# A tuned two-layer scan and FFN kernel: expert masks and sign sums on GpSimd, the sign transposes by DMA, the last slot in two halves

## The chip, the cores and the metric

The kernel runs on one core of a Trainium2 chip. The metric is the device time of one execution in microseconds; the kernel before takes 103.62 us, the median of three runs (103.58 to 103.7). The profile shows the four compute engines of the core (TensorE or PE, VectorE or DVE, ScalarE or ACT, GpSimd or POOL) and SyncE (SP), which here only issues DMAs. Each engine takes its instructions in the order in which the program lists them, and waits on semaphores.

## The reference, cut to what matters

`x` and `F` are (4, 256, 256) in float32, four slots `b` of 256 time steps and 256 channels. There are two layers:

```
x = x + moe(wkv(x, F, F, w0, u0, cond))           # layer 0
x = x + ffn(wkv(x, F, F, w1, u1, cond))           # layer 1

wkv(r, k, v): a_t = a_{t-1}*decay + exp(k_t)*v_t,  b_t = b_{t-1}*decay + exp(k_t)   forward and in reverse
              num = af + ab - ekv + euk*v,  den = bf + bb - ek + euk
              out = sigmoid(r) * num / max(den, 1e-8) * (0.8 + 0.2*tf)
moe(h):       gate = argmax softmax(h Wg^T) over 8 experts; y = 4 * prob * B_e (A_e h), rank 64
ffn(h):       gelu(h W1q^T + b1) W2q^T + b2,   Wq = sign(w) where |w| >= 0.7*mean|w|, else 0
```

`W1` is 1024 x 256 and `W2` is 256 x 1024.

## The kernel before, in words

The channels lie on the partitions, in two chunks `c` of 128, and time lies on the free axis. All work is cut by layer `l` (0, 1) and slot `b` (0 to 3); each engine has its own list of calls, written out by hand, and every order below is that of such a list. There is no planner; semaphores with counts join the lists.

- **Front.** SyncE loads F, x, gate and expert weights, `w1` and `w2` (`w_nat`, 1 MB each). TensorE transposes F, x, A, B against an identity `ident`; between them stand `warm_up` and `keep_warm`, transposes of the identity with no result.
- **wkv of one layer and slot.** On VectorE: `forward(l, b, q)` and `backward(l, b, q)`, two scans each (one per chunk), for the numerator (NUM) and the denominator (DEN); `own_keys`; `add_den`; then ScalarE makes a reciprocal as exp(-ln) (`log_den`, `reciprocal`), and VectorE refines it in one step (`den_times_rec`, then `ratio`, or `refine_rec` and `product` where the numerator comes late). GpSimd does `own_values`, `add_num`, `times_sigmoid` (layer 0) or `times_tanh` (layer 1), `num_times_rec` (needed only for `ratio`) and `seed`, a tiny product that starts the reverse scan.
- **moe of one slot.** TensorE `gate_logits`; VectorE `gate`, `gate_index`; ScalarE `gate_exp`; VectorE `expert_mask`, a reciprocal and two compares of 128x128, one per half of the time steps (lines 882 to 893), with the expert numbers and both scalars in PSUM; TensorE `transpose_mask`; ScalarE `copy_mask`; TensorE `expert_in` into banks 0 and 1; VectorE `select_expert`; TensorE `place_residual` (the slot's x, by matmul with the identity) and `expert_out` on top of it; ScalarE `keep_x1`. `tanh` on ScalarE gives the gate of layer 1 (as tanh, in the table set of gelu; each change of table set is a load).
- **Weights.** ScalarE sums |w| (`abs_sum`), TensorE and VectorE turn that into a threshold, ScalarE writes two sign matrices in bf16, `above` and `below`, 128x2048 per weight matrix. TensorE adds and transposes them in one go, `transpose_weights(k)`, eight groups of eight bf16 matmuls (lines 1182 to 1198) through one PSUM bank, and ScalarE takes each group out as its sign (`evacuate_wT`).
- **ffn of one slot.** The input is split in a high and a low part (`xin_high`, `xin_low`). TensorE `hidden(b, j)`, j = 0 to 3, eight matmuls of 128x128x256; ScalarE `gelus`; `h_high`, `h_low`; TensorE `place_output(b)` (x1 + b2, by matmul with the identity) and `ffn_out(b, j, n)`, four matmuls each; `result` copies the bank out and SyncE stores it.

TensorE's list goes from `warm_up` at line 1266 to the last `ffn_out` at 1372, with `hidden(0, 0)` at 1318. The two lines on which the placements rest are:

```
pe.matmul(bank[Y_BANK][...], x_nat[...], ident[:, :], start=(c == 0 and n == 0), stop=False)      # 1130
pe.matmul(o_region(b, n)[...], x1T(b)[...], ident[:, :], start=(...), stop=False)                 # 1250
```

Of the kernel before, what the change touches and what calls it, by code (L numbers as in the profile page):

```python
# [14 lines left out]
P = 128  # L15
# [9 lines left out]
def adaln_ffn_kernel(nc, x, fside, cond, w_l0, u_l0, A, Bw, Wg, w_l1, u_l1, w1, b1, w2, b2, out):  # L25
# [23 lines left out]
    with ExitStack() as ctx:  # L49
# [9 lines left out]
        identb = sb("identb", [P, P], BF16)  # L59
# [32 lines left out]
        above2 = sb("above2", [P, NC, DFF], BF16)  # L92
        wsum = sb("wsum", [P, 2])
# [7 lines left out]
        gsum = sb("gsum", [P, NI])  # L101
        mask = sb("mask", [P, 2 * NT, P])
# [32 lines left out]
        consts_ready, identb_ready = sem("consts_ready"), sem("identb_ready")  # L135
# [21 lines left out]
        below_ready, above_ready = sem("below_ready"), sem("above_ready")  # L157
        qT_psum, wT_ready = sem("qT_psum"), sem("wT_ready")
# [23 lines left out]

        NEG_AT, IDX_AT, GREC_AT, EXPERT_AT = 4 * ND, 4 * ND + 2, 4 * ND + 2 + NI, P
# [5 lines left out]
        expert_ps = bank[DVE_BANK][:, EXPERT_AT:EXPERT_AT + P]  # L189
# [85 lines left out]

        def seed(eng, l, b, q):
# [25 lines left out]

        def copy_on(eng, dst, src):
# [10 lines left out]
        def h_high(eng, b, j):  # L314
# [24 lines left out]
        def _(sp):  # L339
# [29 lines left out]
            sp.dma_start(w2_nat[:, :, :], w2.rearrange("(n p) f -> p n f", p=P)).then_inc(w_loaded[1], 16)  # L369
            for b in range(NB - 1):  # L370
# [10 lines left out]
        def _(pool):  # L381
# [24 lines left out]

            def factors():
# [36 lines left out]
            seed(pool, 0, 2, NUM)
            add_num(pool, 0, 2)
            times_sigmoid(pool, 2)
            num_times_rec(0, 2)
            seed(pool, 0, 3, NUM)
            own_values(pool, 1, 0)
            add_one(0)  # L450
            seed(pool, 1, 0, NUM)
            add_num(pool, 0, 3)
            times_sigmoid(pool, 3)
            seed(pool, 1, 0, DEN)
            num_times_rec(0, 3)
            add_num(pool, 1, 0)
            times_tanh(pool, 0)
            add_b2(0)
            num_times_rec(1, 0)
            seed(pool, 1, 1, DEN)  # L460
            add_b2(1)
            own_values(pool, 1, 1)
# [935 lines left out]
```

## Time and profile before

| what | value |
|---|---|
| median of three runs | 103.62 us |
| the profiled execution | 102.58 us |
| its span, first to last instruction | 100.8 us |
| PE busy | 93.5 us, 93% |
| DVE busy | 86.7 us, 86% |
| ACT busy | 80.2 us, 80% |
| POOL busy | 66.1 us, 66% |
| DMA | 6.43 MB, nearly all in the first 20 us |

Busy time counts an instruction from its start to its end, and the ends of pipelined matmuls overlap the next ones; how long a group holds its engine is best read from the start of the group to the start of the next. The table's shares are means over two stages that have different limits. A chain of waits is followed back from the last instruction, at each step to what released it.

### The profile page before, as it was taken

The page shows a single profiled execution, that of the slowest core. Times are in us where ns is not written, and L with a number is a line of the kernel's source. Part 1 is how long each engine was busy: PE and PEld are TensorE (multiplying, and loading weights), DVE is VectorE, ACT ScalarE, POOL GpSimd, SP SyncE. Part 2 cuts the span into 40 slices and gives each one's busy share as a digit, 9 for nine tenths or more (in the row PEclk, how much of TensorE's full clock was granted, in tenths as well). Part 3 has the DMA queues.
Part 4 walks back from the last instruction along what each step waited for, and adds up shares of the span by engine and source line. Part 5 has one row for each costly group of instructions (what it writes and reads, how often), then busy time and mean ns, then how long its engine had stood idle before and what let it go on. Part 6 is the DMA issues. An engine that isn't in the chain of part 4 may idle for free. (4 is left out here: it accounts for less than half of the span.)

```text
span 100.8 us, 2134 instructions
## 1 busy us (share of the span) xinstructions
PE 93.5 (93%) x665; PEld 85.0 (84%) x665; DVE 86.7 (86%) x203; ACT 80.2 (80%) x144; POOL 66.1 (66%) x90
## 2 busy tenths in 40 slices
PE   3999779989988999999999999999999999999980
PEld 2688659978878889888888888989999999999970
DVE  3389999999999999999999999999997997883330
ACT  4369999999986679999667499998986899986520
POOL 4058679979984796069868987999980867005310
DMA  1899999700000000000000000000000020200005
GB/s 33 243 292 336 298 228 385 281 3 0 3 0 0 3 0 7 0 0 0 0 3 7 0 0 0 0 0 0 0 7 0 0 104 33 72 7 3 0 0 208
DMA packets 6886, 6.43 MB, mean 64 GB/s; under 512 B 2370, under 2 KB 6492, under 8 KB 6876
## 3 DMA queue, kind: packets, MB, share of 16 engines
q1 hardware_dynamic: 6868, 6.31, 20.2%
q8 instruction: 5, 0.08, 0.3%
q14 instruction: 5, 0.04, 0.1%
q10 hardware_dynamic: 8, 0.00, 0.0%
HBM read 5.26 MB, written 1.05 MB: 63 GB/s over the span
## 5 line engine op out<-in xcount | busy, mean ns | idle before, releaser
L298 POOL TENSOR_TENSOR h_lo<-h,h_hi 128x512 fp32r<-128x512 f32 x9 | 12.3, 1367 | 12.5 <-DVE h_hi L306 7.1
L794 DVE TENSOR_TENSOR_SCAN run<-bank,kv 128x256 f32<-128x256 f32 x32 | 20.1, 674 | 0.2
L1156 PE MATMUL bank<-num,AT 128*128 128x256 f32 x64 | 15.5, 384 | 0.7 <-DVE hm L900 0.5
L1258 PE MATMUL bank<-w2T,h_hi 128*128 128x256 f32 x64 | 15.9, 286 | 0.0
L611 ACT ACTIVATE h<-bank,bT 128x256 f32<-128x256 f32 x32 | 13.1, 478 | 3.2 <-PE bank L1224 2.9
L1224 PE MATMUL bank<-xin_hi,w1T 128*128 128x256 f32 x64 | 15.5, 283 | 0.0
L1258 PE MATMUL bank<-w2T,h_lo 128*128 128x256 f32 x64 | 15.6, 281 | 0.0
L1224 PE MATMUL bank<-xin_lo,w1T 128*128 128x256 f32 x64 | 15.2, 277 | 0.0
L1172 PE MATMUL bank<-hm,BT 128*128 128x256 f32 x64 | 14.6, 381 | 0.0
L1156 PEld LDWEIGHTS bank<-num,AT 128*128 128x128 f32 x64 | 11.6, 190 | 2.2 <-issue 0.9
L1172 PEld LDWEIGHTS bank<-hm,BT 128*128 128x128 f32 x64 | 11.9, 190 | 1.5
L1224 PEld LDWEIGHTS bank<-xin_hi,w1T 128*128 128x128 f32 x64 | 12.0, 188 | 0.6 <-POOL xin_lo L292 0.4
L248 POOL TENSOR_TENSOR num<-num,own 128x512 f32<-128x512 f32 x7 | 8.9, 1278 | 5.2 <-DVE num L828 5.1
L1258 PEld LDWEIGHTS bank<-w2T,h_lo 128*128 128x128 f32 x64 | 12.0, 188 | 0.0
L1258 PEld LDWEIGHTS bank<-w2T,h_hi 128*128 128x128 f32 x64 | 12.0, 188 | 0.0
L1224 PEld LDWEIGHTS bank<-xin_lo,w1T 128*128 128x128 f32 x64 | 12.0, 188 | 0.0
L242 POOL TENSOR_TENSOR own<-own,vs 128x512 f32<-128x512 f32 x8 | 10.2, 1275 | 1.4 <-DVE own L778 1.3
L828 DVE TENSOR_TENSOR_SCAN bank<-bank,run 128x256 f32<-128x256 f32 x16 | 10.2, 681 | 0.0
L828 DVE TENSOR_TENSOR_SCAN num<-bank,run 128x256 f32<-128x256 f32 x16 | 10.1, 671 | 0.0
L405 POOL TENSOR_TENSOR num<-num,run 128x512 f32<-128x512 f32 x5 | 6.4, 1279 | 1.2 <-DVE run L794 0.9
L529 ACT ACTIVATE run<-bank 128x512 f32<-128x512 f32 x8 | 4.8, 605 | 2.9 <-DVE bank L835 2.9
L305 ACT ACTIVATE h_hi<-h 128x512 fp32r<-128x512 f32 x11 | 6.8, 635 | 0.3 <-ACT h L611 0.2
(141 smaller groups left out, 226.1 us busy)
## 6 DMA issues: line engine op xcount, KB each, us to landing
w_nat<-in_L_ffn_w_dram SPq DMA_DIRECT2D x2, 1024.0 KB, 8.5
F_nat<-in_fside_BxSxS_dram SPq DMA_DIRECT2D x4, 256.0 KB, 3.1
x_nat<-in_x_dram SPq DMA_DIRECT2D x4, 256.0 KB, 4.9
out_dram<-outb SPq DMA_DIRECT2D x3, 256.0 KB, 2.1
A_nat<-in_L_ffn_A_dram SPq DMA_DIRECT2D x1, 512.0 KB, 5.6
B_nat<-in_L_ffn_Bw_dram SPq DMA_DIRECT2D x2, 256.0 KB, 6.3
out_dram<-outb SPq DMA_DIRECT2D x2, 128.0 KB, 1.9
wv_rows<-in_L_cond_w_dram SPq DMA_DIRECT2D x2, 1.0 KB
```

The lines of the kernel that those rows point to most:

```text
L242: eng.tensor_tensor(own[:, r, :, NUM, :], own[:, r, :, DEN, :], vs[:, b], ALU.mult).then_inc(ownv_ready[r], 1)
L248: eng.tensor_tensor(num_at(l, b), num_at(l, b), own[:, r, :, NUM, :], ALU.add).then_inc(num_ready[r], 1)
L298: eng.tensor_tensor(h_lo[:, b % 2, 2 * j:2 * j + 2], h32[:, b % 2, 2 * j:2 * j + 2], h_hi[:, b % 2, 2 * j:2 * j + 2].bitcast(F32), ALU.sub ...
L305: return eng.activation(dst, src, ACT.Copy)
L405: pool.tensor_tensor(num_at(l, b), num_at(l, b), run[:, r, :, DEN, :], ALU.mult).then_inc(q_ready[r], 1)
L611: act.activation(h32[:, b % 2, f], bank[g_bank[NJ * b + j]][:, (f % 2) * T:(f % 2 + 1) * T], ACT.Gelu, bias=bT[:, f:f + 1], scale=0.5).the ...
L794: dve.tensor_tensor_scan(run[:, r, c, q], decay_ps[:, l, c, b:b + 1].broadcast_to([P, T]), kv[:, b, c, q], 0.0, ALU.mult, ALU.add).then_in ...
L828: dve.tensor_tensor_scan(into[:, c, ::-1], decay_ps[:, l, c, b:b + 1].broadcast_to([P, T]), run[:, r, c, q, ::-1], 0.0, ALU.mult, ALU.add) ...
L1156: mm = pe.matmul(bank[H_BANK + k][:, (m % 2) * T:(m % 2 + 1) * T], AT[:, c, m * P:(m + 1) * P], num_at(0, b)[:, c], start=(c == 0), stop=( ...
L1172: mm = pe.matmul(bank[Y_BANK][:, o * T:(o + 1) * T], BT[:, m, o * P:(o + 1) * P], hm[:, b % 2, m], start=False, stop=(o == NC - 1 and m == ...
L1224: mm = pe.matmul(bank[g_bank[g]][:, (f % 2) * T:(f % 2 + 1) * T], w1T[:, c, f * P:(f + 1) * P], part[:, b % 2, c], start=(c == 0 and part ...
L1258: mm = pe.matmul(o_region(b, n), part[:, b % 2, f, n * P:(n + 1) * P], w2T[:, f], start=False, stop=(f == NF - 1 and part is h_lo and (n = ...
```

## The change

1. The expert mask moves from VectorE to GpSimd. The expert numbers and scalars now lie in SBUF. The reciprocal stays on VectorE as `gate_reciprocal`.
2. GpSimd adds `above` and `below`, eight pieces of 128x512 in bf16 (`add_signs(w, q)`). SyncE transposes each sum, 128x2048, by one DMA from SBUF to SBUF, and ScalarE evacuates it in two steps of 1024 columns. The 64 matmuls of `transpose_weights` are gone; 28 transposes of the identity (`fill`) and other counts of `warm_up` and `keep_warm` are in.
3. `place_residual` and `place_output` become transposes (`is_transpose=True`).
4. For the last slot of layer 1 everything from the reverse scan of the denominator to `xin_low` is done by chunk, `last_hidden(j, c)` by input chunk, and the last hidden group's gelu, high and low part and output by 128 features. The second chunk's denominator lies in another bank.
5. The lists of all four engines are in a new order. Some calls change the engine: `times_tanh(2)`, `xin_high` of slot 1, `add_num(1, 2)`, several `h_high` and `h_low`, `result(0)`. Ten table loads stand where twelve stood.

```diff
+        def add_signs(w, q):
+            nc.gpsimd.wait_ge(above_ready, w + 1)
+            nc.gpsimd.wait_ge(below_ready, w + 1)
+            part = slice(q * 2 * C, (q + 1) * 2 * C)
+            signs = (above1 if w == 0 else above2)[:, :, :].rearrange(flat)[:, part]
+            nc.gpsimd.tensor_tensor(signs, signs, below[:, part], ALU.add).then_inc(signs_added, 1)
...
+            for w, signs in enumerate((above1, above2)):            # SyncE, ahead of the stores
+                sp.wait_ge(signs_added, 4 * (w + 1))
+                sp.dma_start(signsT[:, w], signs[:, :, :].rearrange(flat), transpose=True).then_inc(signs_moved[w], 16)
...
+            def expert_mask(b):                                     # GpSimd
+                pool.wait_ge(consts_ready, 4 + NE)
+                pool.wait_ge(index_steps, (NT + 1) * (b + 1))
+                pool.wait_ge(grec_ready, b + 1)
+                if b >= 2:
+                    pool.wait_ge(mask_psum, b - 1)
+                for i in range(NT * b, NT * (b + 1)):
+                    pool.tensor_scalar(mask[:, i % (2 * NT)], expert_of[:, :], chosen[:, i:i + 1], prob[:, i:i + 1],
+                                       ALU.is_equal, ALU.mult).then_inc(mask_ready, 1)
...
             def sign_below(k):
                 act.wait_ge(thr_ready, 2)
                 if k:
-                    act.wait_ge(qT_psum, 4)
+                    act.wait_ge(signs_added, 4)
...
             def evacuate_wT(k):
-                act.wait_ge(qT_psum, k + 1)
+                act.wait_ge(signs_moved[k // 2], 16)
...
+                act.activation(dst, src, ACT.Sign).then_inc(wT_ready, 1)      # 128x1024, src = signsT
...
GpSimd's list, from num_times_rec(0, 1) on:
+            expert_mask(0)
+            add_signs(0, 0)
+            add_num(pool, 0, 2)
+            add_signs(0, 1)
             seed(pool, 0, 3, DEN)
+            add_signs(0, 2)
+            add_signs(0, 3)
+            expert_mask(1)
             times_sigmoid(pool, 2)
+            add_signs(1, 0)
             seed(pool, 0, 3, NUM)
+            add_signs(1, 1)
+            seed(pool, 1, 0, NUM)
+            add_signs(1, 2)
+            add_num(pool, 0, 3)
+            add_signs(1, 3)
+            seed(pool, 1, 0, DEN)
+            times_sigmoid(pool, 3)
+            expert_mask(2)
+            num_times_rec(0, 3)
...
ScalarE's list, from reciprocal(0, 1) on (the order after the change):
             gate_exp(0), evacuate_B(0), evacuate_B(1), sign_above(0), sign_below(0), log_den(0, 2), copy_mask(0),
             reciprocal(0, 2), sign_above(1), gate_exp(1), sign_below(1), copy_mask(1), keep_x1(0), log_den(0, 3),
             reciprocal(0, 3), gate_exp(2), evacuate_wT(0), [table] tanh(0), keep_x1(1), tanh(1), evacuate_wT(1),
             copy_mask(2), [table] log_den(1, 0), reciprocal(1, 0), gate_exp(3), evacuate_wT(2), keep_x1(2),
             xin_high(0), evacuate_wT(3), copy_mask(3), log_den(1, 1), reciprocal(1, 1), [table] gelus(0, 0) ...
...
TensorE's list:
-            keep_warm(19)
-            transpose_B(1)
-            keep_warm(27)
+            keep_warm(40)
             gate_logits(0)
+            expert_in(0, 0)
             weight_totals()
+            transpose_B(1)
+            fill(9)
+            place_residual(0)
             expert_in(0, 1)
+            fill(14)
             transpose_mask(0)
+            fill(5)
             gate_logits(1)
...
-            transpose_weights(0)            # and 1 to 7, further down
...
+            expert_out(2)
             expert_in(3, 0)
+            transpose_mask(3)
             expert_in(3, 1)
             hidden(0, 0)
...
+            place_output(3)
+            last_hidden(0, 0)
+            last_hidden(1, 0)
+            last_hidden(0, 1)
+            last_hidden(2, 0)
+            last_hidden(1, 1)
             ffn_out(2, 2, 0)
             ffn_out(2, 2, 1)
+            last_hidden(2, 1)
...
+            last_ffn_out(6, 0)
+            last_ffn_out(6, 1)
+            last_ffn_out(7, 0)
+            last_ffn_out(7, 1)
```

VectorE's list, in the stretch that the prediction adds up (from line 911 on; the order after the change): `seed(0, 0, NUM)`, `own_keys(0, 0)`, `backward(0, 0, DEN)` and `NUM`, `own_keys(0, 2)` and `(0, 1)`, `add_den(0, 0)`, `forward(0, 1, NUM)`, `backward(0, 1, DEN)`, `own_keys(0, 3)`, `den_times_rec(0, 0)`, `add_den(0, 1)`, a seed, `ratio(0, 0)`, `backward(0, 1, NUM)`, `forward(0, 2, NUM)`, `gate(0)`, `forward(0, 2, DEN)`, `thresholds`, and so on to `select_expert(2, 1)`, `(2, 0)`, `add_den(1, 0)`, `forward(1, 1, DEN)`, `gate(3)`, `den_times_rec(1, 0)`, `gate_index(3)`, `gate_reciprocal(3)`, `refine_rec(1, 0)`, a seed, `product(1, 0)`. Ahead of that point it has, unlike before, `own_keys(1, 1)`, `forward(1, 1, NUM)`, and `refine_rec` with `product` for slot 2 of layer 0.

## Rows read from the trace of the kernel before

**Rows 1.** The page: busy time, share of the span and instructions of each engine

```profile
PE 93.5 (93%) x665; PEld 85.0 (84%) x665; DVE 86.7 (86%) x203; ACT 80.2 (80%) x144; POOL 66.1 (66%) x90
```

**Rows 2.** Chain that ended last: start, us, what (the last two: the timeline)

```profile
61.02 0.44 PE bank L1163 x2
97.84 0.42 DVE outb L306
86.37 0.69 DVE L292 TENSOR_TENSOR xin_lo<-sig,xin_hi 128x512 fp32r<-128x512 f32 x1
87.24 0.37 PE L1224 MATMUL bank<-xin_hi,w1T 128*128 128x256 f32 x1
```

**Rows 3.** Stretches: length, busy us of each engine (instructions), clock, DMA

```profile
10.31:54.66 44.35, 41.87 (x293) 37.33 (x293) 43.72 (x117) 38.83 (x66) 33.85 (x37) 1.00 0.22 67
58.70:97.90 39.20, 38.88 (x315) 37.79 (x314) 31.94 (x60) 32.54 (x62) 23.65 (x22) 1.00 0.04 14
15.00:20.00 5.00, 5.00 (x46) 4.91 (x46) 5.00 (x9) 5.00 (x10) 4.92 (x5) 1.00 0.93 344
```

**Rows 4.** Timeline of VectorE: start, us, engine, line, operation, tiles, count

```profile
10.31 1.27 DVE L828 TENSOR_TENSOR_SCAN bank<-bank,run 128x256 f32<-128x256 f32 x2
11.48 0.86 DVE L778 SCALAR_TENSOR_TENSOR own<-ek_raw,bank 128x256 f32<-128x256 f32 x2
...
25.79 0.16 DVE L886 RECIPROCAL bank<-gsum 128x2 f32<-128x2 f32 x1
...
26.73 0.68 DVE L857 SCALAR_TENSOR_TENSOR num<-bank,num 128x512 f32<-128x512 f32 x1
...
51.38 1.26 DVE L794 TENSOR_TENSOR_SCAN run<-bank,kv 128x256 f32<-128x256 f32 x2
...
74.48 0.23 DVE L286 TENSOR_TENSOR run<-run,bank 128x2 f32<-128x2 f32 x2
```

**Rows 5.** Timeline of TensorE: the same columns

```profile
8.96 2.60 PE L1090 MATMUL bank<-ident,x_nat 128*128 128x128 f32 x12
...
15.35 2.24 PE L1041 MATMUL bank<-ident 128*128 128x128 f32 x19
...
24.88 1.05 PE L1130 MATMUL bank<-ident,x_nat 128*128 128x128 f32 x8
25.77 1.89 PE L1156 MATMUL bank<-num,AT 128*128 128x256 f32 x8
...
52.89 3.67 PE L1172 MATMUL bank<-hm,BT 128*128 128x256 f32 x16
56.40 0.22 PE L1196 MATMUL bank<-identb,above 128*128 128x128 bf16 x1
...
56.85 1.95 PE L1156 MATMUL bank<-num,AT 128*128 128x256 f32 x8
```

**Rows 6.** Groups of ScalarE by line and shape: count, busy us, mean ns

```profile
L580 ACT ACTIVATE above<-w_nat,thr 128x2048 bf16<-128x2048 f32 x2 | 4.0, 1990 | 0.0
L595 ACT ACTIVATE w2T<-bank 128x512 fp32r<-128x512 f32 x4 | 2.4, 590 | 0.5 <-PE bank L1197 0.5
L621 ACT ACT_TABLE_LOAD x1 | 1.3, 1283 | 0.0
```

**Rows 7.** Groups of GpSimd by line and shape: the same columns

```profile
L242 POOL TENSOR_TENSOR own<-own,vs 128x512 f32<-128x512 f32 x8 | 10.2, 1275 | 1.4 <-DVE own L778 1.3
L227 POOL TENSOR_SCALAR kv<-ek_raw 128x512 f32<-128x512 f32 x2 | 1.2, 612 | 0.7 <-ACT ek_raw L509 0.6
L231 POOL TENSOR_SCALAR kv<-ek_raw 128x256 f32<-128x256 f32 x2 | 0.8, 400 | 3.2 <-ACT ek_raw L513 3.2
```

**Rows 8.** DMA issues: tiles, count, KB each, median us from issue to landing

```profile
out_dram<-outb SPq DMA_DIRECT2D x3, 256.0 KB, 2.1
A_nat<-in_L_ffn_A_dram SPq DMA_DIRECT2D x1, 512.0 KB, 5.6
B_nat<-in_L_ffn_Bw_dram SPq DMA_DIRECT2D x2, 256.0 KB, 6.3
```

More of the change, by code:

```diff
@@ L450, in _ @@
+            seed(pool, 1, 1, NUM)
             add_one(0)
[L451 to L456, printed above, removed]
-            times_tanh(pool, 0)
[L458 to L462, printed above, removed]
+            times_tanh(pool, 0)
+            expert_mask(3)
@@ L930, in _ @@
-            backward(0, 1, NUM)
-            ratio(0, 0)
-            own_keys(0, 3)
-            own_keys(0, 2)
-            gate(0)
+            seed(dve, 0, 1, NUM)
+            ratio(0, 0)
+            backward(0, 1, NUM)
+            forward(0, 2, NUM)
+            gate(0)
+            forward(0, 2, DEN)
             thresholds()
+            gate_reciprocal(0)
+            seed(dve, 0, 2, DEN)
+            den_times_rec(0, 1)
             gate_index(0)
             backward(0, 2, DEN)
-            den_times_rec(0, 1)
@@ L939, in _ @@
[L939 removed]
+            backward(0, 2, NUM)
+            add_den(0, 2)
             ratio(0, 1)
[L941 removed]
             forward(0, 3, DEN)
+            select_expert(0, 0)
+            den_times_rec(0, 2)
+            gate(1)
             select_expert(0, 1)
[L944 to L947 removed]
+            own_keys(1, 1)
             gate_index(1)
+            gate_reciprocal(1)
+            forward(1, 0, NUM)
@@ L965, in _ @@
+            refine_rec(0, 2)
+            select_expert(1, 0)
+            product(0, 2)
+            add_den(0, 3)
+            backward(0, 3, NUM)
+            gate(2)
+            select_expert(1, 1)
+            forward(1, 0, DEN)
+            forward(1, 1, NUM)
+            gate_index(2)
+            gate_reciprocal(2)
+            den_times_rec(0, 3)
+            own_keys(1, 0)
+            backward(1, 0, DEN)
             backward(1, 0, NUM)
-            backward(1, 0, DEN)
             ratio(0, 3)
+            select_expert(2, 1)
@@ L974, in _ @@
             gate_index(3)
-            ratio(1, 0)
-            own_keys(1, 1)
+            gate_reciprocal(3)
+            refine_rec(1, 0)
+            seed(dve, 1, 1, DEN)
+            product(1, 0)
             backward(1, 1, DEN)
-            own_keys(1, 3)
             add_den(1, 1)
-            own_keys(1, 2)
-            forward(1, 1, NUM)
-            expert_mask(3)
             backward(1, 1, NUM)
-            den_times_rec(1, 1)
             select_expert(3, 0)
             select_expert(3, 1)
+            den_times_rec(1, 1)
+            forward(1, 2, DEN)
             refine_rec(1, 1)
-            forward(1, 2, DEN)
+            own_keys(1, 2)
+            h_high(dve, 0, 0)
             product(1, 1)
-            xin_high(dve, 1)
             backward(1, 2, DEN)
@@ L993, in _ @@
             forward(1, 2, NUM)
-            forward(1, 3, DEN)
+            forward(1, 3, NUM)
+            seed(dve, 1, 2, NUM)
             backward(1, 2, NUM)
             den_times_rec(1, 2)
-            forward(1, 3, NUM)
-            times_tanh(dve, 2)
+            add_num(dve, 1, 2)
             seed(dve, 1, 3, NUM)
+            refine_rec(1, 2)
+            forward(1, 3, DEN)
             seed(dve, 1, 3, DEN)
-            refine_rec(1, 2)
             product(1, 2)
```

459 lines of the change are left out of this document (243 added, 216 removed).

## The prediction

> **What bounds the kernel now.** I read first the busy shares [rows 1]: TensorE is at 93%, VectorE at 86%, both over a span of 100.8 us. Then the chain that ended last [rows 2]: before 61 us it lies on VectorE, from 61.02 to the last matmul on TensorE without a break, and then come the copy and the store. Then the stretches [rows 3]: from 10.31 to 54.66 us VectorE is busy 43.72 of 44.35 us, TensorE 41.87 of it, and part of that is warm-keeping and weight transposes that nobody waits for. So there are two stages. Up to about 58.7 us the clock of the kernel is VectorE's queue; from `hidden(0, 0)` at 58.75 on it is TensorE's own length (38.88 busy of 39.20 us), with VectorE only just ahead: slot 3's `xin_low` runs from 86.37 to 87.06 and the matmul that reads it starts at 87.24 [rows 2].
>
> I work with start-to-start distances, since a duration holds latency that the next instruction overlaps. On VectorE [rows 4]: a pair of scans 1.17 us, `own_keys` 0.78, an operation on 128x512 0.59 to 0.60, an expert mask with its reciprocal 0.94 (25.79 to 26.73). On TensorE [rows 5]: 19 transposes 2.11, so 0.111 each; a placement of four blocks by plain matmul, eight records, 0.89 (24.88 to 25.77); `expert_out` 3.51; `expert_in` 1.78.
>
> **Part one, up to 58.7 us: VectorE's queue.** Between 10.31 us and the end of `ratio(1, 0)` (54.66) the new order has one `own_keys` more (+0.78), one forward pair more (+1.17), two ratios turned into `refine_rec` and `product` (0.60 + 0.65 in place of 0.59, so +1.3 for two), four seeds (+0.45, from the pair of seeds, 0.14 start to start [rows 4], and a wait on the scan), no masks (-2.8 for three) but four reciprocals (+0.4). Sum +1.3: `product(1, 0)` ends at 55.9. It is later, but `forward(1, 1, NUM)` and `own_keys(1, 1)` are then done.
>
> To the second `select_expert` of slot 2 the same count, with `add_den(1, 0)` now behind it (-0.6), gives 51.38 + 1.17 + 0.78 + 0.66 - 2.82 + 0.3 + 0.33 - 0.6 = 51.2. TensorE then does `expert_out(2)`, `expert_in(3, 0)`, a mask transpose and `expert_in(3, 1)`: 51.3 + 3.51 + 1.78 + 0.25 + 1.78 = 58.6. Before it was held to 52.89 by a weight transpose and an `expert_in` [rows 5], and did 0.45 us of weight transposes more, 56.40 to 56.85 [rows 5]. So `hidden(0, 0)` stays at about 58.7. The 3.6 us that the eight weight transposes took (0.45 each) are worth nothing on this path: they are replaced by waiting for VectorE, and 28 filler transposes (3.1 us) stand in such waits. The plain placements before 58.7 that get cheaper are worth nothing for the same reason.
>
> **Part two, from 58.7 us: TensorE's length.** Sixteen hidden groups of 0.92 (14.7), 32 output groups of 0.475 (15.2), `expert_out(3)` 3.5, and five placements, one of the residual and four of the output. As transposes they have four passes of 0.111 in place of eight, 0.45 and a little for the change of type, say 0.48, not 0.85: 2.4. Sum 35.8, end of matmuls at 94.5. The same sum for before is 14.7 + 15.2 + 3.5 + 5 x 0.85 + 0.28 = 37.9, and it took 39.1: 1.2 us were gaps (one of them VectorE's mask, 60.68 to 61.02, which is now made on GpSimd before 55.3). Will VectorE keep ahead? From 55.9: to `product(1, 1)` lie three scan pairs, five operations of 0.6, `own_keys`, `h_high(0, 0)` 0.35 and the product 0.65, 8.3, so 64.2 (before 66.28); to `product(1, 2)` five pairs, four of 0.6, three seeds and the product, 9.2, so 73.4 (before 75.96; `add_num(1, 2)` comes to VectorE, `times_tanh(2)` and slot 1's `xin_high` leave it); `xin_low(2)` to 75.2, wanted by TensorE at 75.8; then the last slot. It has own keys 0.78, its scans 2.35, a bank copy 0.6, two half sums 0.7, two `h_low`, `add_num` and `times_tanh` 2.4, and ten half operations of 0.22 to 0.33 (3.1): the first half is ready at 84.5 and the second at 85.1, where before it was 87.06. TensorE wants the first at 85.2. Every margin is 0.6 us or so: where VectorE slips, the end slips.
>
> **ScalarE.** Twelve table loads become ten (1.28 each [rows 6], -2.6). Eight copies of 512 columns (0.49 each start to start) become four of 1024, from 512 at 0.59 and 2048 at 1.99 [rows 6] about 1.0 each: no change. One mask is later, one `xin_high` more. All of it lies beside the other engines if its waits hold.
>
> **GpSimd.** It gains eight additions of sign matrices and eight mask instructions, and loses two `num_times_rec`, one `add_num`, two `h_low` and some seeds. The trace has no bf16 addition; from the same shape in f32, 1.27 us [rows 7], it is 1.24 start to start. Below it is bounded by the one-input row of 612 ns, above by 2.5 us, two of the f32 additions. I take 1.25, the nearest. A mask of 128x128 lies between 0.2 (128x16) and 0.40 (128x256) [rows 7]; I take 0.27. By queue: VectorE ends `ratio(0, 0)` at 20.8 and then has three scan pairs and a gate before `thresholds`, 25.05; ScalarE's two signs of 1.9 start behind `evacuate_B(1)` at 25.3 and end at 29.2, so GpSimd idles from 28.3 to there. Four additions, one `add_num` and a seed make 35.6. `sign_below(1)` waits for them (35.6 to 37.5); a mask pair and `times_sigmoid(2)` fill that time, and four more additions with `add_num(0, 3)` and two seeds end at 44.1. Behind them wait `times_sigmoid(2)` (ends 37.3, VectorE wants it at 39.4), seed (1, 0, DEN) (44.2, wanted 47.1), `num_times_rec(0, 3)` (47.2, wanted 49.4) and `times_tanh(0)` (52.8, wanted 55.3). About 2 us of cover each: the 10 us are free, just.
>
> **The transposing DMAs.** Each moves 512 KB within SBUF; no row shows one. Below: a plain store of 256 KB lands in 2.1 us. Nearest by size: A_nat, 512 KB, 5.6 us. Above: B_nat, read in pieces of 256 B, takes 6.3 us for 256 KB, so 12.6 for 512 KB [rows 8]. I take 5.6. The first starts at 35.6; ScalarE comes to `evacuate_wT(0)` at 42.8, behind `gate_exp(2)`, whose logits VectorE has at 42.3: 7.2 us of cover. The second starts at 44.1 and is wanted at 53.9: 9.8 us.
>
> The Trainium skill (Advanced Engine Details and Errata, X-Bar Transpose (TRN2)) says that such DMAs go as fast as plain ones; by that they are hidden and the sum stands. The Trainium skill (VectorE: DVE Perf Modes, The three transpose paths) has 1309 ns for one 128x128 block; sixteen in a row would be, an estimate, 21 us, and the kernel would be slower. No row here decides between them.
>
> **Sum.** Matmuls end at 94.5; behind them, as before, 3.0 us of copy and store (97.8 to 100.8 [rows 2]): 97.5. For waits that the sum doesn't see I add 0.7, about half of what the second stage had before: 98.2 us of span. Before, the profiled execution took 102.58, 1.78 more than its span, and the median of the runs is 1.04 above that. So 98.2 + 1.78 + 1.04 = 101.0 us. At best (no gap at all, VectorE 0.5 us earlier) 99.8, with a few small slips 102.3.
>
> **Rivals.** (a) The transposing DMA is slow, chance 0.14: this is the slower side. ScalarE takes its queue in order, so `evacuate_wT(0)` holds tanh(0), tanh(1), `copy_mask(2)` and the reciprocal of slot 0's second layer. `copy_mask(2)` has 2.1 us of cover, so a DMA of D us costs D - 7.2 - 2.1. It eats the gain of 2.6 at D = 11.9. At 12.6 it gives 104.3, at 18 us 109. For it: the data go to other partitions two bytes at a time, unlike any row. Against: 9 us of total cover, over A_nat's 5.6.
>
> (b) GpSimd becomes the bound, chance 0.2, most of it mild. With additions of 1.6 and masks of 0.6 a piece, eight of the first and six of the second bring 2.8 + 2.0 us to `num_times_rec(0, 3)`, over a cover of 2.2: +2.6, no gain, 103.6; with half of that excess, 101.2 plus what else slips, some 102.3. For it: GpSimd was idle only about 10 us between 12 and 75, and gets 10 more. Against: its rows of one shape are all within 1.26 to 1.30.
>
> (c) The transposing placements cost what the matmuls did, or TensorE's clock falls, chance 0.05: 2 us of the gain go, 102.8. TensorE now idles 2.0 us (18.8 to 20.8) between the warm-keeping and `gate_logits(0)`. In the trace 12 transposes at 8.96 took 0.203 each and 19 at 15.35 took 0.111 [rows 5]: a ratio near that of the two levels, 1.2 and 2.4 GHz; from 15 to 20 us the granted clock is 1.00, the higher one [rows 3]. The Trainium skill (TensorE: Matmul & The Clock Gate, Part 4: PE-mode transpose) holds that transposes don't bring the clock up; by that, fillers are no help. The trace disagrees: nothing but transposes and two tiny matmuls ran before 15.35.
>
> **Chances.** Forecast 0.61, (a) 0.14, (b) 0.20, (c) 0.05. Likeliest 101.0, its own range 99.8 to 102.3. The range of 8 in 10 takes in (b) and (c): 99.6 to 103.6. Faster by over 0.2% (what a measurement can tell from no change): forecast and (c), and four fifths of (b), less some for unseen stalls, 0.78; within 0.2%: 0.05; slower: (a) and a remainder of (b), 0.17.
>
> **What would show it.** `hidden(0, 0)` at 58 to 59.5 us; place records four, not eight, each group under 0.55 us; TensorE without gaps behind it, ending at 94.5 to 95.5; GpSimd's sign additions at 1.2 to 1.3 us; a DMA that lands in under 7 us, and no wait of ScalarE at `evacuate_wT`; VectorE's last `xin_low` at 85 to 86. Wrong it is if ScalarE stalls on the DMA, or if VectorE waits for GpSimd between 35 and 56 us.

## The result, and the profile after

The kernel with the change takes 104.84 us (median of 4 runs, 104.29 to 105.12), the kernel before 103.60 beside it (103.51 to 103.70): the ratio is 1.0132, 95% interval [1.0079, 1.0185]. It is slower, by 1.2 us; the forecast was 101.0, with a range that ended at 103.6. The profiled execution took 105.12 us over a span of 103.3. Some executions of a kernel take over 1.5% longer than its fastest one; the medians in this text are of all runs, the ratios leave such runs out.

The page of the kernel after, its busy line by engine (it answers to [rows 1]):

```profile
PE 91.3 (88%) x595; PEld 81.4 (79%) x595; DVE 91.7 (89%) x211; ACT 77.1 (75%) x139; POOL 75.5 (73%) x97
```

TensorE lost 2.2 us of work, as the change has it. VectorE gained 5.0 us (86.7 to 91.7) with eight operations more. Its instructions got longer, and the mean of a group hides that. The timeline of VectorE (start, us, engine, line, operation, tiles, count) shows it at five places:

```profile
24.62 0.13 DVE L998 TENSOR_SCALAR thr<-bank 128x2 f32<-128x2 f32 x1
24.79 0.66 DVE L1000 TENSOR_SCALAR thr<-thr 128x2 f32<-128x2 f32 x1
...
34.71 1.11 DVE L980 CAST chosen<-idx 128x2 f32<-128x2 uint32 x1
...
75.47 0.69 DVE L963 TENSOR_TENSOR sig<-bank,num 128x512 f32<-128x512 f32 x1
76.08 2.18 DVE L306 TENSOR_TENSOR h_lo<-h,h_hi 128x512 fp32r<-128x512 f32 x2
78.18 1.77 DVE L300 TENSOR_TENSOR xin_lo<-sig,xin_hi 128x512 fp32r<-128x512 f32 x1
...
86.06 1.77 DVE L265 TENSOR_TENSOR num<-num,sig 128x512 f32<-128x512 f32 x1
```

The same operations in the kernel before (its timeline of VectorE; `xin_low` took 0.69 [rows 2]):

```profile
23.45 0.17 DVE L907 TENSOR_SCALAR thr<-thr 128x2 f32<-128x2 f32 x1
...
33.46 0.16 DVE L880 CAST bank<-idx 128x2 f32<-128x2 uint32 x1
...
75.96 1.28 DVE L298 TENSOR_TENSOR h_lo<-h,h_hi 128x512 fp32r<-128x512 f32 x2
...
82.29 0.68 DVE L265 TENSOR_TENSOR num<-num,sig 128x512 f32<-128x512 f32 x1
```

The second threshold takes 0.66 us instead of 0.17; the cast of the index takes 1.11, and 0.17 where it is shortest in this same run; the pair of subtractions `h_low` takes 2.18 instead of 1.28; `xin_low` and `times_tanh` take 1.77 instead of 0.69 and 0.68. That is 0.49 + 0.94 + 0.90 + 1.08 + 1.08 = 4.5 us, and none of it shows as a wait, since no semaphore is involved. GpSimd's timeline in the same stretches says what ran beside:

```profile
24.15 1.27 POOL L236 TENSOR_TENSOR kv<-kv,vs 128x512 f32<-128x512 f32 x1
...
33.53 2.26 POOL L282 TENSOR_TENSOR above<-above,below 128x512 bf16<-128x512 bf16 x2
...
76.06 1.04 POOL L274 TENSOR_TENSOR x_nat<-x_nat,bT 128x512 f32<-128x512 f32 x1
77.72 1.68 POOL L306 TENSOR_TENSOR h_lo<-h,h_hi 128x512 fp32r<-128x512 f32 x1 [0.61 <-ACT h_hi L321]
...
85.76 1.53 POOL L306 TENSOR_TENSOR h_lo<-h,h_hi 128x512 fp32r<-128x512 f32 x1 [3.06 <-ACT h_hi L321]
```

Each long VectorE operation ends just after GpSimd's operation plus the work it has to do itself. The threshold starts at 24.79 and ends at 25.45, and GpSimd's product ends at 25.42; the cast ends at 35.82, GpSimd's second addition at 35.79; `times_tanh` ends at 87.83, 0.54 us behind GpSimd's `h_low`. At 77.72 GpSimd's `h_low` (1.30 at 74.81, where it stands free) is itself held to the end of VectorE's pair, takes 1.68 and ends at 79.40; VectorE's `xin_low` stood behind it and ends at 79.95. The operations which are held read two tiles in SBUF, or copy or scale from SBUF to SBUF. The one at 75.47 has one input in a PSUM bank and takes its usual 0.69 with GpSimd busy beside it, as all the scans do. I call this **being held**, and the theory that it is the main loss theory A.

The Trainium skill (SBUF — State Buffer, SBUF: two separate sides) states this rule: VectorE and GpSimd share one pair of SBUF ports, which a VectorE operation needs if it has two SBUF inputs or runs in a two-port mode; whichever begins first has it for the whole instruction, and the other fully blocks. The rows above agree: 0.49 to 1.08 us of being held, with nothing shared out. Which operations run in a two-port mode no trace here shows. The prediction didn't weigh that rule.

Where TensorE waits for it (timeline of TensorE; the last column is the idle time ahead and what ended it; the rows answer to [rows 2, 5]):

```profile
51.28 1.06 PE L1259 MATMUL bank<-WgT,num 128*128 128x8 f32 x8 [1.15 <-DVE num L957]
52.48 5.41 PE L1291 MATMUL bank<-hm,BT 128*128 128x256 f32 x16
...
61.21 0.47 PE L1323 MATMUL bank<-xin_hi,w1T 128*128 128x256 f32 x1
...
80.00 0.39 PE L1323 MATMUL bank<-xin_hi,w1T 128*128 128x256 f32 x1 [1.08 <-DVE xin_lo L300]
...
90.54 0.38 PE L1336 MATMUL bank<-xin_hi,w1T 128*128 128x256 f32 x1 [0.82 <-DVE xin_lo L933]
```

The two gaps of the second stage, 1.08 and 0.82 us, both end on an `xin_low`. The last one on VectorE was at 86.37 to 87.06 before [rows 2], and now:

```profile
90.73 0.42 DVE L933 TENSOR_TENSOR xin_lo<-sig,xin_hi 128x256 fp32r<-128x256 f32 x1
```

The second thing to see above is the 5.41 us of `expert_out(2)`, 3.67 before [rows 5]. The stretches (length, busy us of each engine and instructions, granted clock, DMA; compare [rows 3]) give the reason:

```profile
50.00:55.00 5.00, 3.72 (x19) 3.08 (x18) 4.97 (x13) 3.16 (x6) 4.84 (x7) 0.88 0.01 2
55.00:60.00 5.00, 5.00 (x21) 4.17 (x20) 4.76 (x15) 3.41 (x9) 3.70 (x5) 0.78 0.00 0
61.20:100.20 39.00, 37.10 (x294) 35.53 (x292) 34.87 (x66) 31.32 (x61) 22.48 (x20) 1.00 0.05 15
```

From 54 to 57 us the granted clock was 0.50, the lower of the two levels (1.2 GHz); ahead of it TensorE had idled 1.15 us at 50.1 and 0.90 us at 40.3. `expert_in(3, 1)` came later by it, and VectorE waited 0.56 us for it:

```profile
61.60 0.69 DVE L993 TENSOR_TENSOR hm<-bank,mask_rows 128x512 f32<-128x512 f32 x1 [0.56 <-PE bank L1275]
```

Theory C says that the clock is the main loss. Theory B is the prediction's rival (b), GpSimd as the bound: its masks and additions are (groups: count, busy us, mean ns, idle before; beside [rows 7])

```profile
L282 POOL TENSOR_TENSOR above<-above,below 128x512 bf16<-128x512 bf16 x8 | 9.2, 1154 | 0.3 <-ACT below L628 0.3
L434 POOL TENSOR_SCALAR mask<-expert_of,chosen,prob 128x128 f32<-128x128 f32 x8 | 6.3, 793 | 1.0 <-DVE prob L986 1.0
```

and the transposing DMA, the prediction's (a), landed in (count, median us; beside [rows 8])

```profile
signsT<-above SPq DMA_TRANSPOSE x2, 4.3
```

### The profile page after: what moved, and what is told of

It is laid out like the page before. It is cut to its first block, busy times and chain, and to the rows that moved or that the text cites. A ratio compares the mean times of both kernels' runs of the same rounds, so it can differ in the third digit from the quotient of the medians.

```text
span 103.3 us, 2006 instructions
## 1 busy us (share of the span) xinstructions
PE 91.3 (88%) x595; PEld 81.4 (79%) x595; DVE 91.7 (89%) x211; ACT 77.1 (75%) x139; POOL 75.5 (73%) x97
## 4 chain that ended last, share of the span: by engine, by line
DVE 32%; PE 30%; issue 17%; POOL 12%; ACT 2%; DVEq 2%; DMA 1%; POOLq 0%
PE bank L1291 9%; DVE run L838 7%; PE bank L1275 5%; PE bank L1371 5%; PE bank L1336 4%; PE bank L1184 3%; POOL own L242 3%; DVE num L874 3%; POOL num L254 2%; POOL num L248 2%; PE bank L1147 2%; DVE own L822 2%; DVE bank L874 2%; DVE h_lo L306 2%; DVE bank L892 2%
## 5 line engine op out<-in xcount | busy, mean ns | idle before, releaser
L1291 PE MATMUL bank<-hm,BT 128*128 128x256 f32 x64 | 16.3, 413 | 0.1
L306 POOL TENSOR_TENSOR h_lo<-h,h_hi 128x512 fp32r<-128x512 f32 x7 | 9.6, 1376 | 6.8 <-ACT h_hi L321 4.0
L1323 PE MATMUL bank<-xin_hi,w1T 128*128 128x256 f32 x48 | 12.0, 290 | 1.1 <-DVE xin_lo L300 1.1
L1323 PE MATMUL bank<-xin_lo,w1T 128*128 128x256 f32 x48 | 11.5, 279 | 0.0
L1323 PEld LDWEIGHTS bank<-xin_hi,w1T 128*128 128x128 f32 x48 | 9.0, 188 | 1.5 <-DVE xin_lo L300 1.3
L282 POOL TENSOR_TENSOR above<-above,below 128x512 bf16<-128x512 bf16 x8 | 9.2, 1154 | 0.3 <-ACT below L628 0.3
L1323 PEld LDWEIGHTS bank<-xin_lo,w1T 128*128 128x128 f32 x48 | 9.0, 188 | 0.0
L874 DVE TENSOR_TENSOR_SCAN bank<-bank,run 128x256 f32<-128x256 f32 x14 | 8.9, 677 | 0.2
L248 POOL TENSOR_TENSOR num<-num,own 128x512 f32<-128x512 f32 x6 | 7.6, 1272 | 0.7 <-DVE num L874 0.6
L434 POOL TENSOR_SCALAR mask<-expert_of,chosen,prob 128x128 f32<-128x128 f32 x8 | 6.3, 793 | 1.0 <-DVE prob L986 1.0
```

Of the source, the lines that this page charges most:

```text
L248: eng.tensor_tensor(num_at(l, b), num_at(l, b), own[:, r, :, NUM, :], ALU.add).then_inc(num_ready[r], 1)
L282: nc.gpsimd.tensor_tensor(signs, signs, below[:, part], ALU.add).then_inc(signs_added, 1)
L306: eng.tensor_tensor(h_lo[:, b % 2, 2 * j:2 * j + 2], h32[:, b % 2, 2 * j:2 * j + 2], h_hi[:, b % 2, 2 * j:2 * j + 2].bitcast(F32), ALU.sub ...
L434: pool.tensor_scalar(mask[:, i % (2 * NT)], expert_of[:, :], chosen[:, i:i + 1], prob[:, i:i + 1], ALU.is_equal, ALU.mult).then_inc(mask_r ...
L874: dve.tensor_tensor_scan(into[:, c, ::-1], decay_ps[:, l, c, b:b + 1].broadcast_to([P, T]), run[:, r, c, q, ::-1], 0.0, ALU.mult, ALU.add) ...
L1291: mm = pe.matmul(bank[Y_BANK][:, o * T:(o + 1) * T], BT[:, m, o * P:(o + 1) * P], hm[:, b % 2, m], start=False, stop=(o == NC - 1 and m == ...
```

## Experiments

The kernel after has a median of 104.84 us and a ratio of 1.0132 to before. The experiments ran on other chips, where the kernel before had medians of 103.4 to 103.9 us but spread over 102.3 to 105.1. So a distance from after is given in two ways, by the medians and by the ratios; they differ by up to 1 us, and less than that is not told apart across chips. In the expectations theory A is the one above; theory B is the rival that the run in question tests, and only in 1 and 3 is that GpSimd as the bound.

**1. One line of GpSimd's list moved (a_b2_late).** In the kernel after:

```diff
             h_low(pool, 1, 0)
-            add_b2(2)
             h_low(pool, 1, 2)
+            add_b2(2)
```

> The changed kernel with one call moved in GpSimd's list: add_b2(2) behind h_low(1, 2). No work is taken away. Theory A (an operation of VectorE with two inputs in SBUF waits until a running GpSimd operation has ended): in the changed kernel the h_low on VectorE at 76.08 stood 0.9 us longer than its usual 0.69 beside add_b2(2), and xin_low(2) at 78.18 took 1.77 beside h_low(1, 2). With add_b2(2) away the first h_low takes 0.69 and the two h_low and xin_low(2) are through before GpSimd's h_low(1, 2) starts, so all three take 0.7: VectorE's last xin_low comes 1.5 to 2.0 us earlier, span 101.3 to 101.8, about 103.1 us. Theory B (GpSimd's queue is simply too long, its work late): its length is unchanged, so under 0.3 us is gained, and the three durations stay.

Measured: 102.36 us (101.06 to 102.91, 11 runs), ratio 0.9946 [0.9905, 0.9986]. That is 2.5 us under after by the medians and 1.9% by the ratios, from one moved line that adds and takes away no work. VectorE's timeline:

```profile
74.75 1.28 DVE L306 TENSOR_TENSOR h_lo<-h,h_hi 128x512 fp32r<-128x512 f32 x2
75.95 0.69 DVE L300 TENSOR_TENSOR xin_lo<-sig,xin_hi 128x512 fp32r<-128x512 f32 x1
...
82.74 0.69 DVE L265 TENSOR_TENSOR num<-num,sig 128x512 f32<-128x512 f32 x1
```

The `h_low` pair and `xin_low` have their old lengths again, which is 1.98 us and what the move was to give. The rest of the 4.0 us between the two spans (99.3 against 103.3) isn't the move's: this profile is of the fastest of the eleven runs (101.06; the others took 102.1 to 102.9). In it `times_tanh` is free too (1.08), which I hadn't planned; the granted clock is 0.998, and VectorE's wait of 0.56 is gone; and the cast took 0.19 instead of 1.11, by the luck of starting just ahead of the moment at which one of GpSimd's two additions ended and the next one hadn't begun (VectorE, then GpSimd):

```profile
34.71 0.19 DVE L980 CAST chosen<-idx 128x2 f32<-128x2 uint32 x1
```

```profile
33.71 2.28 POOL L282 TENSOR_TENSOR above<-above,below 128x512 bf16<-128x512 bf16 x2
```

Two other casts were held by 0.25 and 0.32 more than in the kernel after, and 1.98 + 1.08 + 0.92 + 0.56 - 0.57 is 4.0. The pair and `xin_low` are what theory A foretold; the queue is as long as it was, so that GpSimd is too slow overall (theory B) doesn't fit.

**2. The clock held up by fillers (a_filled).**

```diff
+            fill(9)
             gate_logits(2)
...
+            fill(11)
             gate_logits(3)
```

> The changed kernel with 9 and 11 transposes of the identity ahead of gate_logits(2) and gate_logits(3), where TensorE idled 0.90 and 1.15 us. Theory A: the idle stretches are what let the granted clock fall to 0.50 from 53.9 to 57 us, so that expert_out(2) took 5.24 us in place of 3.5; with them filled the clock stays at 1.00 all through, expert_out(2) takes 3.5, VectorE's 0.56 us wait for expert_in(3, 1) goes, and 0.6 to 0.9 us are gained (the one run of the changed kernel at clock 1.000 had a span of 102.4, the others 102.9 to 103.3): about 104.2 us. Theory B (the clock fell for another reason than these gaps, and comes back each time): nothing, 104.8. If the clock's share were most of the loss, it would be 102.5 or less.

Measured: 104.52 us (103.64 to 105.46, 4 runs), ratio 1.0114 [0.9999, 1.0229]; granted clock 1.000 in the profiled run (0.984 in the slowest of the four), and `hidden(0, 0)` starts at 59.62 instead of 61.21. The clock is cured, and the time moves little. As much is held as in the kernel after (3.29 + 0.68 here, 2.18 + 1.77 there, and `times_tanh` in both), so VectorE gets back only its wait of 0.56 us: its last `xin_low` ends at 90.61 instead of 91.15, and the span is 102.7 instead of 103.3. VectorE:

```profile
75.52 3.29 DVE L306 TENSOR_TENSOR h_lo<-h,h_hi 128x512 fp32r<-128x512 f32 x2
78.74 0.68 DVE L300 TENSOR_TENSOR xin_lo<-sig,xin_hi 128x512 fp32r<-128x512 f32 x1
...
85.53 1.77 DVE L265 TENSOR_TENSOR num<-num,sig 128x512 f32<-128x512 f32 x1
```

0.6 us of span is the lower end of what was expected; the medians differ by 0.3, and the interval is too wide to say more than that the clock alone isn't the loss.

**3. The masks back on VectorE (a_masks_back).** GpSimd loses its eight mask instructions, and VectorE makes them from PSUM operands, as before; the index is cast into PSUM again too:

```diff
             num_times_rec(0, 1)
-            expert_mask(0)                # GpSimd's list; masks 1 to 3 likewise
             add_signs(0, 0)
...
-                dve.tensor_copy(chosen[:, both], idx8[:, both, 0]).then_inc(index_steps, 1)
+                dve.tensor_copy(bank[DVE_BANK][:, IDX_AT + NT * b:IDX_AT + NT * (b + 1)], idx8[:, both, 0]).then_inc(index_steps, 1)
...
+                    dve.tensor_scalar(mask[:, i % (2 * NT)], expert_ps, bank[DVE_BANK][:, IDX_AT + i:IDX_AT + i + 1],
+                                      bank[DVE_BANK][:, GREC_AT + i:GREC_AT + i + 1], ALU.is_equal, ALU.mult).then_inc(mask_ready, 1)
```

> The changed kernel with the expert masks made on VectorE again, from PSUM, as before the change, each behind its index and reciprocal. VectorE gets four pairs of 0.67 us (2.7), GpSimd loses four of 1.56. Theory A (VectorE's length sets the end, and the casts of the expert index to SBUF cost it 0.94 + 0.08 us of waiting for GpSimd, which with a PSUM output go away): 2.7 - 1.0 = 1.7 us slower less what GpSimd's lighter list gives elsewhere, 105.5 to 106.5 us. Theory B (GpSimd's list is the bound): 2 us faster, 103.

Measured: 106.83 us (106.67 to 107.93, 4 runs), ratio 1.0418 [1.0315, 1.0521]: 2.0 us worse than after by the medians, 2.9% by the ratios. With 6.3 us taken off GpSimd and 3.0 us put on VectorE (eight of 415 ns, overlapping a little) the kernel is slower, so GpSimd's load is not the bound, and theory B is refuted. The `h_low` pair (3.27) and `times_tanh` (1.77) are still held, `xin_low` (0.68) isn't: 3.95 us for pair and `xin_low` together, as in the kernel after. The four casts into PSUM take 0.16 to 0.17, so 3.0 us of masks less 1.0 of held casts is the 2.0 that the medians show.

**4. The placements alone (place_only).** In the kernel before, both placements get `is_transpose=True` and nothing else changes.

```diff
-    nc.tensor.matmul(..., x_nat[...], ident[:, :], start=..., stop=False)
+    nc.tensor.matmul(..., x_nat[...], ident[:, :], start=..., stop=False, is_transpose=True)
```

> The kernel before with nothing but is_transpose=True in place_residual and place_output. Both theories: a placement takes about 0.45 us in place of 0.81 to 0.89, four records in place of eight; five of them lie in the stretch from 58.7 us on, where TensorE's own length counted: up to 2.0 us faster, 101.7. If VectorE, which there was only just ahead (0.2 us at slot 3's xin_low), takes over as the bound, only 0.2 to 0.8 us faster, 103.0.

Measured: 102.54 us (101.83 to 103.45, 10 runs), ratio 0.9954 [0.9901, 1.0008]. That lies between the two times expected; the interval ends just above 1, so whether it is faster stays open. Its VectorE timeline, and TensorE's at the same place:

```profile
86.47 0.69 DVE L292 TENSOR_TENSOR xin_lo<-sig,xin_hi 128x512 fp32r<-128x512 f32 x1
```

```profile
87.21 0.39 PE L1224 MATMUL bank<-xin_hi,w1T 128*128 128x256 f32 x1 [0.52 <-DVE xin_lo L292]
```

That `xin_low` started at 86.37 before: shortening TensorE does not bring VectorE's last slot forward, and TensorE now waits 0.52 us for it.

**5. PSUM operands instead of SBUF ones (a_psum).** In the kernel after, the two small operations of the first stage get one operand in a PSUM bank:

```diff
-    dve.tensor_copy(chosen[:, both], idx8[:, both, 0])
+    dve.tensor_tensor(chosen[:, both], idx8[:, both, 0], <a column of -1 in PSUM>, ALU.mult)   # expert_of holds -e
...
-    dve.tensor_scalar(thr[:, 1], thr[:, 0], -1.0, None, ALU.mult)
+    dve.tensor_scalar(thr[:, 1], bank[WTOT_BANK][:, 0:2], 1.0 / (DFF * C), -0.7, ALU.mult, ALU.mult)
```

> The changed kernel with two small operations of VectorE given an operand in PSUM: the copy of the expert index to SBUF becomes a product of the index with the column of -1 in PSUM (expert numbers are negated to match), and the second threshold is worked out from the totals in PSUM, not from the first threshold. Theory A (an operation of VectorE that has two inputs in SBUF, or copies SBUF to SBUF, waits for the GpSimd operation that is running): the two no longer wait; 1.11, 0.25 and 0.66 us become about 0.17 each, VectorE is 1.5 us earlier at 36 us, and the long h_low, xin_low and times_tanh further on, which are not touched, may stay: 0.5 to 1.5 us faster than the changed kernel, about 103.8 us. Theory B (any small operation of VectorE can be held, whatever its operands): durations of 0.5 to 1.1 us remain, no gain.

Measured: 103.65 us (103.40 to 104.04, 10 runs), ratio 1.0061 [1.0021, 1.0101]: 1.2 us under after by the medians, 0.7% by the ratios. VectorE:

```profile
24.58 0.15 DVE L1000 TENSOR_SCALAR thr<-bank 128x2 f32<-128x2 f32 x1
...
34.15 0.16 DVE L980 TENSOR_TENSOR chosen<-idx,bank 128x2 f32<-128x2 uint32 x1
...
74.48 2.18 DVE L306 TENSOR_TENSOR h_lo<-h,h_hi 128x512 fp32r<-128x512 f32 x2
```

0.66 and 1.11 us became 0.15 and 0.16, with the same work on GpSimd beside them; the operations that were left as they were are still held. With GpSimd busy at the same time, the place of the operand decides. That fits a shared way into SBUF; a slowdown of whatever VectorE does beside GpSimd it doesn't fit.

**6. Moved line and fillers (a_b2_fill).** The edits of 1 and 2 together.

> add_b2(2) behind h_low(1, 2) and the 20 filler transposes together. Theory A: the clock's part adds to the moved call's, 0.3 to 0.8 us under its 102.36, so 101.8; granted clock 1.00 from 50 to 60 us in every run. If the clock doesn't matter once VectorE sets the end: 102.4.

Measured: 102.08 us (101.06 to 102.32, 4 runs), ratio 0.9876 [0.9791, 0.9961]. The clock was 1.000 in the profiled run, but 0.982 and 0.983 in two of the others, one of them the fastest, so "in every run" was missed. `times_tanh` is held again (1.78). This kernel and that of experiment 2 (on another chip) differ in the moved line alone, and both profiles have a clock of 1.000 and a held `times_tanh`: spans of 100.4 and 102.7, 2.3 us for the line, of which 2.01 are the pair and `xin_low` (1.28 + 0.68 against 3.29 + 0.68).

**7. All three (a_best).** The edits of 1, 2 and 5 together.

> add_b2(2) behind h_low(1, 2), the filler transposes, and both PSUM operands. Theory A: all three gains, as far as TensorE's length allows: hidden(0, 0) at 58.7, span 98 to 98.8, about 101.0 us, where the blind forecast stood. Theory B: as a_b2_fill.

Measured: 100.87 us (100.25 to 100.91, 6 runs), ratio 0.9775 [0.9719, 0.9832]. It beats both kernels. The profiled run is one of the two fastest; the spans of the other four are 99.1. Its VectorE timeline and one stretch of it:

```profile
75.15 0.69 DVE L300 TENSOR_TENSOR xin_lo<-sig,xin_hi 128x512 fp32r<-128x512 f32 x1
...
81.94 0.69 DVE L265 TENSOR_TENSOR num<-num,sig 128x512 f32<-128x512 f32 x1
...
84.34 0.59 DVE L928 CAST xin_hi<-sig 128x256 fp32r<-128x256 f32 x1
...
85.84 0.43 DVE L933 TENSOR_TENSOR xin_lo<-sig,xin_hi 128x256 fp32r<-128x256 f32 x1
```

```profile
58.00:95.30 37.30, 36.87 (x294) 35.51 (x292) 33.49 (x69) 32.21 (x62) 23.39 (x20) 1.00 0.05 16
```

TensorE is busy 36.87 of 37.30 us again; of VectorE's second stage one operation is held, the cast at 84.34, by 0.3 us.

**8. The collision put into the kernel before (b_collide).** There `add_b2(2)` moves behind `h_low(pool, 1, 0)`, next to VectorE's pair.

```diff
             seed(pool, 1, 2, DEN)
-            add_b2(2)
...
             h_low(pool, 1, 0)
+            add_b2(2)
             h_low(pool, 1, 2)
```

> The kernel before with add_b2(2) moved in GpSimd's list from behind seed(1, 2, DEN) to behind h_low(1, 0), so that it runs beside VectorE's h_low(0, 3) at 75.96. Theory A: that h_low, 0.68 us before, takes 1.2 to 1.7 us. VectorE had 0.56 us of waiting ahead of xin_low(2) and 0.75 ahead of the last den_times_rec, so the end moves by 0 to 0.4 us: 103.4 to 103.8. Theory B (the long durations belong to the changed kernel's other edits, its new order of lists or its DMA): all h_low of VectorE stay at 0.69.

Measured: 103.34 us (102.53 to 105.30, 4 runs), which can't be told from before (103.49): two runs took 102.5 and two 104.1 and 105.3, and there is no interval for it. What the experiment shows is in its trace. VectorE's pair is held there too, by 0.64 us (1.28 before), beside GpSimd's addition:

```profile
75.64 1.92 DVE L298 TENSOR_TENSOR h_lo<-h,h_hi 128x512 fp32r<-128x512 f32 x2
```

```profile
75.37 1.03 POOL L274 TENSOR_TENSOR x_nat<-x_nat,bT 128x512 f32<-128x512 f32 x1
```

So being held isn't tied to the change; before, one collision falls into slack. There GpSimd was idle from 75.7 to 78.37, while VectorE did its `h_low` pair and waited 0.56 us for ScalarE.

**9. and 10. The clock's price once little is held (a_late_psum, a_best_again).** a_best without its fillers, and a_best once more on the same chip.

> The kernel of a_best without its 20 filler transposes ahead of gate_logits(2) and gate_logits(3), so with the late add_b2(2) and the PSUM operands alone. It prices the clock by itself once the held VectorE operations are gone. Theory A (held operations are most of the loss): the two edits' gains add up, and the fillers are worth little: 101.2 to 101.7 us, expert_out(2) still 4.4 to 5.4 us long with a granted clock below 1.00 between 50 and 56 us, hidden(0, 0) at 58.8 to 59.6. Theory C (the clock is worth more than the held operations left): 102.3 us or more, 1.5 us above a_best, and TensorE's later stage waits for VectorE no less than in a_best.

> The kernel of a_best once more, on the chip on which a_late_psum runs, so that the two are compared under the same conditions. 100.7 to 101.2 us, granted clock 1.000, expert_out(2) at 3.7 us; by theory A at most 0.8 us under a_late_psum, by theory C 1.5 us or more.

Measured: 101.35 us (100.53 to 101.92, 6 runs), ratio 0.9792 [0.9711, 0.9873], without the fillers; 101.07 (100.37 to 101.52, 6 runs), ratio 0.9778 [0.9694, 0.9862], with them. The two can't be told apart. Yet without them TensorE's timeline has the long `expert_out(2)` and `hidden(0, 0)` starts at 60.13, later than expected:

```profile
50.21 1.06 PE L1259 MATMUL bank<-WgT,num 128*128 128x8 f32 x8 [1.06 <-DVE num L957]
51.41 5.41 PE L1291 MATMUL bank<-hm,BT 128*128 128x256 f32 x16
```

With them it starts at 58.22: 1.9 us on TensorE at that point, and 0.3 us between the medians. The two profiled runs don't price the clock by themselves, since they differ in `times_tanh` as well: it was free in a_late_psum (0.68) and held in a_best_again, the same code as 7, where it was free. VectorE's timeline of a_best_again, and GpSimd's:

```profile
82.10 1.77 DVE L265 TENSOR_TENSOR num<-num,sig 128x512 f32<-128x512 f32 x1
```

```profile
81.82 1.51 POOL L306 TENSOR_TENSOR h_lo<-h,h_hi 128x512 fp32r<-128x512 f32 x1 [1.82 <-ACT h_hi L321]
```

and GpSimd's in 7:

```profile
81.66 2.12 POOL L306 TENSOR_TENSOR h_lo<-h,h_hi 128x512 fp32r<-128x512 f32 x1 [1.82 <-ACT h_hi L321]
```

In both runs GpSimd's `h_low` starts 0.28 us ahead of `times_tanh` and behind an `h_low` of VectorE that is still running. In one GpSimd goes next and VectorE is held by 1.08; in the other VectorE goes on and GpSimd is held by 0.8. While VectorE's earlier `h_low` runs neither can begin; which of the two comes next, no row decides. The span of a_best_again was 99.3 us, that of 7 was 98.5.

What prices the clock best is one row: in each of the three profiles where it fell at 51 to 57 us (after, a_psum, a_late_psum) VectorE waited 0.56 us for `expert_in(3, 1)`, and in none of those where it stayed at 1.00. Theory C, as the main loss, falls.

## Why the prediction was wrong

**The step that failed** is the count of VectorE's queue, "Will VectorE keep ahead?", with its "Every margin is 0.6 us or so: where VectorE slips, the end slips". It added up durations measured in the kernel before, as if an operation took the same time whatever GpSimd does. The change filled just the gaps of GpSimd in which they had been free. Also, it moved the index and the reciprocal from a PSUM bank to SBUF (before, the index was cast into the bank in 0.16), so the cast could be held as well. By milestones, in us:

| | forecast | after | a_best |
|---|---|---|---|
| `product(1, 0)` ends | 55.9 | 57.1 | 55.6 |
| `hidden(0, 0)` starts | 58.7 | 61.2 | 58.05 |
| `product(1, 1)` ends | 64.2 | 66.4 | 64.2 |
| `product(1, 2)` ends | 73.4 | 76.2 | 74.0 |
| `xin_low(2)` ends | 75.2 | 79.95 | 75.84 |
| last `xin_low` ends | 85.1 | 91.15 | 86.27 |
| span | 98.2 | 103.3 | 98.5 |

Read down the second column against the first: +1.2 (threshold and cast held, 1.43 together, the rest absorbed), +2.2 (0.56 of it a wait for `expert_in(3, 1)`, late by the clock), +2.8 (0.6 of it my count, which is short in a_best too), +4.75 (the `h_low` pair 0.90 and `xin_low` 1.08), +6.05 (`times_tanh` 1.08). TensorE then ends 9.1 us behind the last `xin_low`, both in after and in a_best; the forecast had 9.4 and 0.7 for unseen waits, which is why the span is off by 5.1 and not by 6.05. The third column is near the forecast with most held operations and the clock taken away, 100.87 against 101.0 us. It is not the kernel that was forecast, and part of the nearness is luck: its first stage is 0.65 us ahead of the forecast, its second 0.85 longer.

**Part one.** The order was read rightly; the masks did leave VectorE, and that was worth 2 to 3 us (experiment 3), net of the casts that came to be held.

**Part two, TensorE.** The placements were read rightly: four records, 0.35 to 0.44 from start to start where nothing is waited for, forecast 0.48. The sum is short: in a_best TensorE takes 37.35 us from the start of `hidden(0, 0)` to its last matmul, with 0.34 of waiting, where the forecast had 35.8; several groups of eight matmuls take 1.0 to 1.1, not 0.92. Being right about TensorE was worth little, as VectorE sets the end (experiments 4, 9).

**GpSimd.** Additions 1.15 us, forecast 1.25. The masks were mis-sized: 0.79 each, not 0.27; above both durations of one-input operations that I took as bounds. At 0.5 x 8 = 4 us more, no wait of VectorE's followed. "About 2 us of cover each: the 10 us are free, just" counted semaphores and was right about those; it was wrong that the 10 us are free.

**Transposing DMAs.** 4.3 us, forecast 5.6, fully hidden: rival (a) didn't occur. The Trainium skill (Advanced Engine Details and Errata, X-Bar Transpose (TRN2)), by which such DMAs go as fast as plain ones, agrees with the row: 4.3 against 5.8 for the plain load of A_nat. The 21 us that the prediction estimated for sixteen blocks in a row did not come.

**Rivals.** (b) had the engine right and the mechanism wrong: it priced GpSimd's queue, which experiment 3 refutes as the bound. Of (c), the clock did fall, at 54 to 57 us and not where I looked (18.8 to 20.8 us, granted clock 1.00, TensorE idle for 0.8 of these 2.0), and cost VectorE 0.56 us. The prediction's argument there leans on 0.203 us a transpose at 8.96 against 0.111 at 15.35, as near the ratio of the two levels; but in the kernel before the granted clock was 1.00 in the first stretch as well (same columns as [rows 3]), so those rows don't show the clock, and why the first twelve took 0.203 stays open:

```profile
8.96:11.40 2.44, 2.36 (x14) 1.96 (x14) 2.36 (x5) 2.44 (x5) 1.90 (x7) 1.00 1.06 319
```

No rival had the port, so the slower side got 0.17, and the range missed by 1.2 us.

**What stays open:** why `times_tanh` is held in one run and not in the next, with starts of the same distance; whether the placements alone gain; and what lets the clock fall. Idle time ahead of it isn't enough: in the profiled run of a_b2_late TensorE idled 1.39 us at the same gate and the clock stayed at 1.00, while behind 1.06 us in a_psum and a_late_psum it fell; and in two other profiles it fell elsewhere, at 15 to 19 us (a_masks_back) and at 23 to 27 us (place_only).

## What to carry to other kernels

Before work goes to GpSimd, list VectorE's operations that read two SBUF tiles, or copy from SBUF to SBUF, and lay GpSimd's new busy time over them. Where they overlap, one of the two waits until the other's instruction has ended, and neither the waits nor the chain show it, only a duration above the group's usual one. The cures that worked here are cheap: one operand in PSUM, or one GpSimd operation moved by a place in its list. A stage with 0.6 us of margin on each step needs the price of an overlap in its range.

## What the hardware showed that I had not expected

- A VectorE cast of 128x2 took 1.11 us beside two bf16 additions on GpSimd, and 0.16 with a PSUM operand: the smallest operation waits until the other engine's instruction has ended.
- The granted clock fell to 0.50 for 3 us behind idle times of only 0.90 and 1.15 us. With 20 filler transposes ahead of the two gates the mean clock of a run was 0.995 or more in 15 of 20 runs (experiments 2, 6, 7, 10), without them in 8 of 31 (after, experiments 1, 5, 9).
- GpSimd is held as well: its `h_low` of 1.29 us took 2.12 in a_best, beside two operations of VectorE, and VectorE lost nothing.
- A GpSimd compare-and-multiply of 128x128 with two per-partition scalars takes 790 to 802 ns (8 of them), longer than a one-input operation on 128x512 (612 [rows 7]).
- A transposing DMA of 512 KB within SBUF lands in 4.3 us, less than the plain load of A_nat (5.8 in this kernel, 5.6 before [rows 8]).
